# Expert weights fetched as two parts, each with its own semaphore, and a new table of steps for every engine

## What is computed

```python
# layer 1: an RWKV block (a scan over the tokens, then a channel mix of width 512)
x = x + rwkv(layernorm(x))
# layer 2: attention with 16 heads of 8 channels, then a mixture of 8 experts, 2 for each token
h = layernorm(z)
attn = softmax(q @ k.T / sqrt(8)); z = z + (attn @ v) @ Wo
m = layernorm(z); wts, idx = top_k(softmax(m @ Wg), 2)
ye = gelu(m @ W1[e] + b1[e]) @ W2[e] + b2[e]          # for the two experts e of a token
z = z + sum(wts * ye)
x = x + z
```

## Time and profile before

| | |
|---|---|
| runs of the kernel before | 984.49, 981.62, 976.50 us; median 981.62 |
| the profiled execution | 989.37 us, of which 987.7 us span |
| busy share | TensorE 83%, VectorE 67%, ScalarE 61%, GpSimd 43% |
| DMA | 116.77 MB, mean 118 GB/s; granted clock 0.905 on average |

### The profile page before, as it was taken

How to read it: one execution, slowest core, us unless ns; L and a number is a source line. 1 busy time by engine, 2 the same in 40 slices (tenths; PEclk the granted TensorE clock), 3 DMA queues, 4 the chain that set the end, 5 groups by cost and what they waited for, 6 DMA issues and landing times. The chain is left out here.

```text
span 987.7 us, 15981 instructions
## 1 busy us (share of the span) xinstructions
PE 820.5 (83%) x5416; PEld 516.9 (52%) x5416; DVE 665.6 (67%) x1341; ACT 600.2 (61%) x1016; POOL 424.9 (43%) x543
## 2 busy tenths in 40 slices
PE   3558898878898999788989998988898888898772
PEld 1444445434555654345556555654565555478771
DVE  4538858886879688868886878687867576223112
ACT  2123446644787687447876887677768876556341
POOL 5544333534553455464534553454556013115263
PEclk9675798888899999898999999998999998699797
DMA  6500321991522300015233321053223320558793
GB/s 196 169 12 9 122 98 49 292 347 45 179 90 89 101 21 9 12 33 180 89 100 103 108 86 57 30 183 97 89 80 123 119 80 27 181 188 298 236 309 95
DMA packets 106286, 116.77 MB, mean 118 GB/s; under 512 B 7983, under 2 KB 89310, under 8 KB 106206
## 3 DMA queue, kind: packets, MB, share of 16 engines
q1 hardware_dynamic: 102110, 107.36, 34.3%
q0 software_dynamic: 4096, 8.40, 2.6%
HBM read 77.24 MB, written 38.49 MB: 117 GB/s over the span
## 5 line engine op out<-in xcount | busy, mean ns | idle before, releaser
L1456 DVE TENSOR_REDUCE QA<-psB 128x2 f32<-128x1024 f32 x256 | 311.9, 1219 | 124.0 <-PE psB L1143 121.7
L943 ACT ACTIVATE PT<-psB 128x1024 f32<-128x1024 f32 x256 | 261.9, 1023 | 134.3 <-PE psB L1159 130.4
L1159 PE MATMUL psB<-Q,KT 32*128 32x512 f32 x512 | 134.4, 521 | 34.0 <-ACT PT L943 20.6
L1143 PE MATMUL psB<-KT,Q 24*128 24x512 f32 x512 | 136.9, 530 | 22.6 <-DVE QA L1456 21.7
L1171 PE MATMUL psV<-PT,VA 128*32 128x512 f32 x1024 | 148.5, 654 | 0.6
L1236 PE MATMUL psA<-MX,WB 128*128 128x128 f32 x792 | 109.4, 290 | 31.2 <-ACT H L971 19.7
L971 ACT ACTIVATE H<-psA,WB 128x128 f32<-128x128 f32 x396 | 109.8, 376 | 33.3 <-PE psA L1236 31.3
L1236 PEld LDWEIGHTS psA<-MX,WB 128*128 128x128 f32 x792 | 100.0, 202 | 39.4 <-issue 28.3
L1246 PEld LDWEIGHTS psY<-WB,H 128*128 128x128 f32 x792 | 96.8, 194 | 27.8 <-ACT H L971 16.8
L1159 PEld LDWEIGHTS psB<-Q,KT 32*128 32x128 f32 x512 | 49.7, 191 | 117.1 <-ACT PT L943 75.3
L1246 PE MATMUL psY<-WB,H 128*128 128x128 f32 x792 | 107.6, 282 | 0.0
(11 more groups left out here) (198 smaller groups left out, 1360.0 us busy)
## 6 DMA issues: line engine op xcount, KB each, us to landing
WB<-w_rows SPq DMA_DIRECT2D x99, 578.0 KB, 5.7
pairs<-XT SPq DMA_DIRECT2D x2, 5120.0 KB, 18.5
outs<-XT SPq DMA_DIRECT2D x2, 5120.0 KB, 33.5
XT<-pairs SPq DMA_DIRECT2D x99, 64.0 KB
outs<-YT SPq DMA_DIRECT2D x99, 64.0 KB
w_rows<-WB SPq DMA_DIRECT2D x8, 578.0 KB, 3.3
X<-in_L_attn_x_dram SPq DMA_DIRECT2D x8, 256.0 KB, 3.0
H<-in_L_ffn_W_dram SPq DMA_DIRECT2D x8, 256.0 KB, 3.9
```

The costliest lines, as they stand in the source:

```text
L943: act.activation(PT[:, (c % 2) * G + j:(c % 2) * G + j + 2, :], psT, ACT.Exp, scale=SCALE).then_inc(t_taken.sem, 1)
L1143: pe.matmul(dst[:, h, :], chunk(Q1[r, g, :], c), KT[r, g, :], start=True, stop=True).then_inc(s_full.sem, 1)
L1159: pe.matmul(psT[:, h, :], chunk(KT[r, g, :], c), Q2[r, g % 2, :], start=True, stop=True).then_inc(t_full.sem, 1)
L1456: dve.tensor_reduce(QA[:, c, g * G + j:g * G + j + 2, RM], plain(b, i), AX_X, ALU.max).then_inc(s_taken.sem, 1)
```

## The change

The two biases change places, so that the block is W1, b1 (516 numbers) and W2, b2 (640 numbers). `weights_in` becomes `first_layer_in` and `second_layer_in`, each with three DMAs (258 KB and 320 KB). The first waits tile by tile until window w's hidden products have been read by gelu; the second waits for `y_taken` as before. `hidden` and `gelu` wait for `w1_in`, `expert` now waits for `w2_in`.

```diff
-    W2, B1, B2 = F, 2 * F, 2 * F + NF
+    B1, W2, B2 = F, F + NF, 2 * F + NF
-            def weights_in(w):
+            def first_layer_in(w):
                 if w == 0:
                     for e in range(E - 4, E):
                         sp.wait_ge(w_out[e % 4], 16 * (e // 4 + 1))
+                for i, n in enumerate(members(w)):
+                    if w >= 2:
+                        u = use(members(w - 2)[min(i, len(members(w - 2)) - 1)], "h")
+                        sp.wait_ge(u.taken, u.after)
+                    sp.dma_start(WB[:, ring(n), 0:W2], WS[experts[n]][:, 0:W2]).then_inc(w1_in[ring(n)], 16)
+
+            def second_layer_in(w):
                 if w >= 2:
                     sp.wait_ge(y_taken.sem, y_taken.at(w - 2, 1))
                 for n in members(w):
-                    sp.dma_start(WB[:, ring(n), :], WS[experts[n]]).then_inc(w_in[ring(n)], 16)
+                    sp.dma_start(WB[:, ring(n), W2:], WS[experts[n]][:, W2:]).then_inc(w2_in[ring(n)], 16)
...
-            TILE = {3: (tile_step(0, next_rows),), 7: (tile_step(0, next_weights),), 9: (tile_step(0, rows_out),)}
-            GROUP = {-4: (begin(0),), 0: (begin(1),)}
+            TILE = {7: (tile_step(0, next_rows),), 9: (tile_step(0, next_first),), 10: (tile_step(0, next_second),),
+                    15: (tile_step(0, rows_out),)}
+            GROUP = {1: (begin(0),), 3: (begin(1),)}
...
-            END = {4: (gather(0, 0),), 8: (gather(0, 1), gather(0, 2),), 16: (gather(0, 3),), 17: (gather(1, 0),),
-                   31: (gather(1, 1),), 32: (gather(1, 2), gather(1, 3),)}
+            END = {9: (gather(0, 0),), 10: (gather(0, 1),), 12: (gather(0, 2), gather(0, 3),), 22: (gather(1, 0),),
+                   38: (gather(1, 1),), 40: (gather(1, 2),), 44: (gather(1, 3),)}
...
             def expert(n):
                 i = within(n) % WIN
                 pe.wait_ge(use(n, "h").taken, use(n, "h").after)
+                pe.wait_ge(w2_in[ring(n)], landed(n))
```

More of the change, by code:

```diff
@@ L262, in build @@
         ys_zero = sem("ys_zero_0"), sem("ys_zero_1")
[L268 to L275, removed]
+        USES = [(0.5, "core", "kt2"), (1.5, "core", "qt2"), (1.9, "core", "q2_0"), (3.5, "core", "v"), (6.5, "post", "ctx"),
+                (7, "post", "out"), (7.5, "tail", "wo"), (9, "core", "kt3"), (9.9, "core", "q2_1"), (10.5, "tail", "xc"),
+                (11.5, "core", "qt3"), (14, "post", "rows"), (14.5, "tail", "kk0"), (15, "tail", "kk1"), (15, "tail", "kk2"),
+                (16, "post", "logits"), (17, "tail", "kk3"), (17.9, "core", "q2_2"), (18, "tail", "rr"),
+                (18.5, "post", "rank"), (19, "tail", "kv"), (22.5, "tail", "zh"), (23, "tail", "k"), (23, "tail", "q"),
+                (24, "tail", "kt0"), (24, "tail", "qt0"), (25, "head", "ZA"), (25.9, "core", "q2_3"), (26, "tail", "kt1"),
+                (27.5, "head", "K"), (30, "head", "V"), (30.5, "tail", "qt1"), (31, "head", "R")]
+        TILE_USES = [(3.5, "first", "x"), (5, "first", "h"), (5, "second", "h"), (5.5, "third", "h")]
         a_full = sem("a_full_0"), sem("a_full_1")
@@ L369, in build @@
         xt_in = [sem(f"xt_in_{i}") for i in range(2)]
-        w_in = [sem(f"w_in_{i}") for i in range(2 * WIN)]
+        w1_in = [sem(f"w1_in_{i}") for i in range(2 * WIN)]
+        w2_in = [sem(f"w2_in_{i}") for i in range(2 * WIN)]
         y_out = [sem(f"y_out_{i}") for i in range(2)]
@@ L572, in next_rows, with next_first, next_second @@
                     rows_in(window(n) + 2)
-            def next_weights(n):
+            def next_first(n):
                 if goes_on(n):
-                    weights_in(window(n) + 2)
+                    first_layer_in(window(n) + 2)
+            def next_second(n):
+                if goes_on(n):
+                    second_layer_in(window(n) + 2)
             def rows_out(n):
@@ L587, in step @@
                     rows_in(WINDOW_0[group] + i)
-                    weights_in(WINDOW_0[group] + i)
+                    first_layer_in(WINDOW_0[group] + i)
+                    second_layer_in(WINDOW_0[group] + i)
                 return step
@@ L821, in gather_rows @@
                                                 bass.IndirectOffsetOnAxis(IDX[:, b % 6, k, c:c + 1], 0)).then_inc(gathered[k][c], 16)
[L823 to L827, removed]
-            END = {4: (gather(0, 0),), 8: (gather(0, 1), gather(0, 2),), 16: (gather(0, 3),), 17: (gather(1, 0),),
-                   31: (gather(1, 1),), 32: (gather(1, 2), gather(1, 3),)}
+            HEAD = {25.5: (head_norm, head_shift,), 30.5: (head_sigmoid,)}
+            TAIL = {1.5: (side,), 2: (wkv_out,), 8.5: (wkv_sum, norm_1, tail_shift,), 10.5: (residual,), 16.5: (square,),
+                    17.5: (sigmoid,), 22.5: (norm_2,), 31.5: (residual_2,)}
+            CORE = {11: (keep,)}
+            POST = {9: (c_norm,), 17.5: (positions,), 22: (scatter(0),), 23: (scatter(2),)}
+            END = {9: (gather(0, 0),), 10: (gather(0, 1),), 12: (gather(0, 2), gather(0, 3),), 22: (gather(1, 0),),
+                   38: (gather(1, 1),), 40: (gather(1, 2),), 44: (gather(1, 3),)}
             def turn(n):
@@ L968, in gelu @@
                     act.wait_ge(y_full.sem, y_full.at(n - 4, 1))
-                act.wait_ge(w_in[ring(n)], landed(n))
+                act.wait_ge(w1_in[ring(n)], landed(n))
                 for f in range(NF):
@@ L1231, in hidden @@
                 pe.wait_ge(use(n - i, "x").taken, use(n - i, "x").after)
-                pe.wait_ge(w_in[ring(n)], landed(n))
+                pe.wait_ge(w1_in[ring(n)], landed(n))
                 u = use(n, "h")
```

49 lines of the change are left out of this document (25 added, 24 removed).

## The result

The changed kernel takes 992.35 us (median of four runs, 989.15 to 993.58), the kernel before 982.35 us beside it (four runs, 976.50 to 984.49). The ratio is 1.0082, with a 95% interval from 1.0048 to 1.0115. The profiled execution is one of 993.03 us with 991.3 us of span, 3.7 us more than that of before.

What follows compares the result with a forecast made beforehand. TensorE's list was taken to set the pace, so only its standing time counts. Terms -1 - 2.5 + 2.2 + 2.5 + 1.7 = +2.9 us on the median of 981.62 us gave 984.5 us, range 973 to 994.

Steps and rivals of the forecast that it cites:

- rival 2: SyncE's queue sets the end: three more issues a window make landings slip; +13 us, 994; chance 0.22.
- The split with the core running: Weight fetches while the core runs: three more issues a window, 1.6 us, cost nothing; 0.
- SyncE's waits hide it: nothing: SyncE while the core runs: its round grows from 7.36 to about 9 us, within a window's 24.7 us; no cost.
- The last windows: Group 4's five windows: earlier first halves against full DMA engines and a full queue; -1 us, ends -7 and +4.
- the first layers of group 4 wait less but the second layers wait for `w2_in`: Expected sign in the changed kernel's profile of the last windows, along with a SyncE round near 9 us.
- Gathers: GpSimd, turn 6: gathers moved behind K let MV come earlier; -2.5 us, ends 0 and -4.3.
- EV, K and the two D, 1.25 us each, run from 676.6: GpSimd, turn 6: these products end at 681.6, the gathers at 691.2, the sum's products at 693.8, when MV could come.
- ZA: TensorE, turns 2 and 4: ZA ahead of an expert tile waits 1.3 us instead of 0.18; +2.2 us, ends 0 and 2.6.
- VA: ScalarE: VA behind the exponential delays the gelus' table load, 0.5 us in each of five turns; +2.5 us, ends 0.5 and 3.
- KA: TensorE, turn 5: the 1.11 us wait at KA goes but returns at the next ZA; counted 0, end -1.1.
- Positions: GpSimd's routing: `positions` 1.85 us later, 0.33 us left over in each of turns 1 to 5; +1.7 us, ends 0 and 3.
- The other moves ... count as zero: Moves of x and v, kk2, rows and kk0, two bias columns: swap neighbours that wait for nothing in the trace; 0.

Runs made afterwards that it cites:

- experiment 1: Kernel before with only the weight fetch split in two, both parts issued at SyncE's old slot, all tables as before: 987.27 us, ratio 1.0049.
- experiment 11: Kernel before with only the weight fetch split in two, but whole blocks for the last group's five windows: 1023.94 us, ratio 1.0046.
- experiment 3: Changed kernel with GpSimd's gathers back at their old slots, nothing else: 994.22 us, ratio to the kernel before 1.0123.
- experiment 5: Changed kernel with TensorE's transpose of ZA behind the expert tile again and ScalarE's copy of VA at slot 4 again: 990.09 us, ratio to the kernel before 1.0066.
- experiment 6: Changed kernel with the routing steps (VectorE's rank and map of tiles, GpSimd's sigmoid) at their old places: 985.51 us, ratio to the kernel before 1.0023.
- experiment 8: Changed kernel with gathers of groups 0 and 1 in GpSimd's idle stretches and the scan's sum at slot 4: 989.01 us, ratio to the kernel before 1.0064.
- experiment 2: Changed kernel with weights fetched as whole blocks on one semaphore again, all new tables kept: 986.30 us, ratio to the kernel before 1.0051.

## Why the prediction was right or wrong

Forecast +2.9 us, to 984.5. The profiled executions differ by +3.7, the medians by +8 (the ratio) to +10, and the measured 992.35 us lies near the upper end of the range and near rival 2's 994, whose mechanism is not what the runs show. That the profiled pair comes out so near the sum is luck twice over. The profiled execution of before was itself 7.0 us above its median, that of the changed kernel 0.7. And within the pair two things that the sum left out nearly cancel: turn 1 wins 3.5 us, and the wait at SEL in turn 3 costs 3.4. Term by term:

**The split with the core running, 0.** The profile of experiment 1 agrees: no turn is longer by more than 0.3 us. The medians speak against it: without the last group's split the ratio was 1.0046 [1.0020, 1.0073] in experiment 11. The step "SyncE's waits hide it: nothing" is thus not borne out, and where the cost arises stays open.

**The last windows, -1.** The sign is wrong, and one of the prediction's own signs of being wrong came: a window of group 4 took 9 us and more (9.60 us at full clock, 11.80 at 0.71). SyncE's round was sized well (8.96 us forecast; the last full round is 8.6 to 9.3 in the changed kernel and the experiments 1, 3, 5, 6 and 8, and 7.0 to 7.5 with whole blocks). But "the first layers of group 4 wait less but the second layers wait for `w2_in`" came out only in part: no second layer of group 4 waited for `w2_in` (one of group 3's last window did, 0.93 us), and instead the rows waited 0.7 to 1.5 us four times from 917 us on. From the first issue of rows in group 4 to the last bias, the profiles apart from the third chip's give 49.2 us on average with whole blocks (four) and 50.1 with halves (six), and from there to the end 18.2 against 18.7 to 19.0: a cost of 1.4 to 1.7 us. Only the second part is clear of the spread: the first is 48.4 to 50.0 us with whole blocks and 48.3 to 52.1 with halves. That is rival 2's mechanism at about a sixth of its price. The medians of experiments 1 and 2 put the split at 3 to 5 us; where the rest lies stays open. The estimate that a half block comes 0.8 us sooner than a whole one was too small: it lands 2.4 us sooner in the median (3.3 against 5.7 us), and that still didn't help.

**Gathers, -2.5.** Failed as costed, though experiment 3 bears out the sign. MV comes 102.67 us after that of turn 5 (595.50 to 698.17), not 100.5. The step "EV, K and the two D, 1.25 us each, run from 676.6" took each engine's durations as its own. R came at 674.56, the four products Z took 3.85 us (3.25 before), and EV started at 678.99, as late as before. From there to the sum EV+K, forecast at 14.6 us, pass 16.45: the first gather took 1.92 us and the second D 1.82, and the eight gathers held the sum until 695.44; TensorE then waits 1.49 us for MV. Nor could MV have come at 693.8 without more: in the kernel before it starts right behind VectorE's reciprocal (695.36 + 1.74), which in the changed kernel ends at 694.75. What the move does win is another thing: the scan AA falls from 3.51 to 1.22 us and slot 2 from 5.5 to 2.8 us. Slot 6 takes it back, 6.9 us instead of 3.7. And the move's price in turn 3, 3.4 us at SEL, was not looked for. The medians put the move at some 4 us in the new tables (experiment 3, 1.0123 against 1.0082, with intervals that overlap); the trace gives it 2.8 us, in turn 6.

**ZA, +2.2.** The wait is as forecast (1.27 us), and undone by experiment 5. The price was mis-sized: some 0.3 us of each of the two turns, since TensorE then waits less for what follows.

**VA, +2.5.** Right in its mechanism, a little large: 0.42 us more wait in turn 4, and with VA at its old place (experiment 5) slot 5 is 0.4 to 0.5 us shorter in each of turns 2, 4, 5 and 6. Against the kernel before slot 5 is not longer (4.9 us, 5.0 before); what is longer there is slot 4 (2.3 us, 1.85 before), in every turn from 2 to 5 and with VA at its old place too.

**KA, 0.** As forecast: the 1.11 us at KA in turn 5 went and came back at ZA, in slot 22 (1.15 to 1.90 us) and slot 25 (0.40 to 1.26 us).

**Positions, +1.7.** Borne out by the trace, if a little small: 2.5 us of waits go in experiment 6, 0.8 of them in turn 1. Its measured gain is 1.4 or 5.8 us, as one takes the changed kernel at 1.0037 or 1.0082.

**"The other moves ... count as zero."** This failed. Slots 0 to 4 take 12.6 us instead of 11.5 in turns 2, 3 and 5 and 11.9 instead of 11.5 in turn 4, 3.8 us in all, of which slot 31 gives back 0.4 us in turns 2, 4 and 5: the scan AA is held 0.6 us longer beside D, with waits of 0.49 us at slot 0 and 0.6 to 0.85 at slot 3 (turns 3 and 5). In turn 1 the scan fell from 2.23 to 1.22 us and a wait of 1.98 us for ZM went, most of the 3.5 us won there. These small moves weren't tried one by one, so that they are the cause is read from the trace, not shown by an experiment.

## What to carry to other kernels

Where VectorE and GpSimd both work on the on-chip memory, a duration is no property of an instruction: compare the same instruction over the turns, and where one takes 3.5 us and its sister 1.2, look at what GpSimd runs beside it before you move either. Find one that ran with nothing beside it as well: the 0.72 us that looked like PR's own duration were 0.19 and a wait. A step that is put ahead of a row of GpSimd's products pushes them together, and the smallest VectorE product behind then waits for all of them. Splitting a transfer in two won nothing here: on a queue without rest it lengthened rounds by its issues, and what stood behind, the rows, came late. And know the spread of a kernel's executions before you set one profile against one other: here 8 us lay between runs of the same kernel, more than the forecast change.

## What the runs showed of the hardware

VectorE's scan AA took 1.22 us with gathers beside it and 1.75, 2.38 and 3.5 us beside GpSimd's products; the product PR took 0.19 us alone, 0.72 us beside one square and 4.17 us beside four. In return GpSimd's second D took 2.06 us beside the scan, 1.27 without it. Gathers on GpSimd came every 1.25 us. Three more issues on SyncE's queue lengthened the last full round by 1.1 to 2.3 us (8.6 to 9.3 us against 7.0 to 7.5). A block of 578 KB landed 5.7 us after its issue in the median, its parts of 320 and 258 KB after 4.7 and 3.3 us. One chip of three ran all these kernels some 3.5% longer, with single stops of 8 to 12 us at first layers in the last windows of all four profiles, while turns 2 to 5 were as long as on the others within about 1 us.
